# One decoder layer on one core: the attention's steps written in a different order on every engine, W1 loaded early, the last inputs loaded in two parts

## The reference: one decoder layer

```python
def _L0_attn_ref(x, w_qkv, w_out, b_out):        # 16 heads of 8 columns
    qkv = jnp.einsum('bsd,ed->bse', x, w_qkv)
    ...
    q = _apply_rope(q, cos, sin)
    k = _apply_rope(k, cos, sin)
    scores = jnp.einsum('bhsd,bhtd->bhst', q, k) * SCALE
    attn = jax.nn.softmax(scores, axis=-1)
    out = jnp.einsum('bhst,bhtd->bhsd', attn, v)
    out = out.transpose(0, 2, 1, 3).reshape(b, s, d)
    return jnp.einsum('bsd,ed->bse', out, w_out) + b_out

# xattn: an autocorrelation of x and ctx over all batches gives 11 shifts and weights
# ffn: 8 experts (128 -> 256 -> 128), the best 2 of each row, then a layer norm
x = _layernorm(x + _L0_attn_ref(x, ...), axis=-1)
x = _layernorm(x + _L0_xattn_ref(x, ctx_1024, ctx_1024, ...), axis=-1)
x = _layernorm(x + _L0_ffn_ref(x, ...), axis=-1)
```

## Time and profile before

| | |
|---|---|
| median of 3 runs | 232.21 us (231.36 to 234.07) |
| the profiled execution's own time | 231.93 us |
| its span in the profile | 230.1 us |
| PE, weight loads of PE | 214.4 us (93%), 184.0 us (80%) |
| DVE, ACT, POOL | 181.3, 142.5, 111.4 us busy |
| chain of work that ended last | PE 70%, DMA 10%, ACT 6%, DVE 6% |

### The profile page before, as it was taken

The page is one execution under the profiler, slowest core; times in us unless marked ns, Lnnn a source line. Parts: engine busy times, 40 slices in busy tenths (PEclk is TensorE's granted clock), DMA queues, the critical chain, the costliest instruction groups (busy, mean ns, idle before and its releaser), DMA issues.

```text
span 230.1 us, 7213 instructions
## 1 busy us (share of the span) xinstructions
PE 214.4 (93%) x2724; PEld 184.0 (80%) x2724; DVE 181.3 (79%) x622; ACT 142.5 (62%) x248; POOL 111.4 (48%) x219
## 2 busy tenths in 40 slices
PE   7988899999999989998899999999999999999970
PEld 7866677767777666778787999789988999889970
DVE  0688998989899899677744778897798868874885
ACT  2587889989999995574489400891029610596112
POOL 5289879979989995423630400252002600030484
PEclk9999999999999999999999999999999999999996
DMA  5941353975565551610000000001000100001001
GB/s 151 284 119 37 61 107 65 130 156 109 122 139 93 48 91 18 164 36 1 3 0 0 0 3 1 0 3 46 4 0 0 46 3 1 0 4 46 1 16 34
DMA packets 32454, 12.32 MB, mean 54 GB/s; under 512 B 19906, under 2 KB 32290, under 8 KB 32418
## 3 DMA queue, kind: packets, MB, share of 16 engines
q1 hardware_dynamic: 31554, 11.48, 24.2%
q10 hardware_dynamic: 864, 0.36, 0.6%
HBM read 6.33 MB, written 1.05 MB: 32 GB/s over the span
## 4 chain that ended last, share of the span: by engine, by line
PE 70%; DMA 10%; ACT 6%; DVE 6%; issue 4%; SPq 2%; POOL 1%; DVEq 0%; ACTq 0%
PE bank L1328 13%; PE scoreT_pair L1328 12%; PE score_pair L1298 11%; PE scoreT_pair L1298 8%; DMA qT_all<-stack 6%; DMA qT_all<-mT 4%; PE bank L965 4%; PE bank L1042 3%; PE scoreT_pair L997 2%; PE bank L1046 2%; PE scoreT_pair L945 2%; SPq L348 2%; PE bank L1059 2%; ACT early L737 2%; PE score_pair L981 1%
## 5 line engine op out<-in xcount | busy, mean ns | idle before, releaser
L1385 DVE TENSOR_REDUCE rowmax<-score_pair 128x8 f32<-128x1024 f32 x32 | 39.0, 1218 | 4.1 <-PE score_pair L981 3.1
L608 POOL TENSOR_TENSOR ve<-mv,table 128x4 f32<-128x4 f32 (+1 forms) x12 | 3.3, 276 | 78.1 <-DVE mv L1745 60.2
L737 ACT ACTIVATE early<-scoreT_pair 128x1024 f32<-128x1024 f32 x32 | 32.9, 1028 | 6.6 <-PE scoreT_pair L997 6.4
L1328 PE MATMUL bank<-w,early 128*128 128x128 f32 x256 | 30.1, 276 | 0.0
L1328 PE MATMUL scoreT_pair<-w,early 128*128 128x128 f32 x256 | 29.9, 275 | 0.0
L1328 PEld LDWEIGHTS bank<-w,early 128*128 128x128 f32 x256 | 29.5, 192 | 0.3
L1328 PEld LDWEIGHTS scoreT_pair<-w,early 128*128 128x128 f32 x256 | 29.2, 192 | 0.0
L1298 PE MATMUL score_pair<-x2T_part,w_part 128*128 128x512 f32 x108 | 28.4, 397 | 0.0
L880 ACT ACTIVATE early<-score_pair,b 128x512 f32<-128x512 f32 x38 | 26.0, 691 | 3.2 <-PE score_pair L1298 2.6
L1042 PE MATMUL bank<-early,v_pad 128*32 128x128 f32 x512 | 26.5, 279 | 0.4 <-DVE attnT L1401 0.3
L1046 PE MATMUL bank<-early,head_ones 128*32 128x128 f32 x512 | 25.8, 273 | 0.0
(11 more groups left out here) (229 smaller groups left out, 469.6 us busy)
## 6 DMA issues: line engine op xcount, KB each, us to landing
w<-in_w SPq DMA_DIRECT2D x8, 256.0 KB, 3.6
x_ext<-in_x SPq DMA_DIRECT2D x4, 256.0 KB, 6.5
qT_all<-mT SPq DMA_DIRECT2D x32, 32.0 KB, 2.3
early<-in_xT SPq DMA_DIRECT2D x3, 256.0 KB, 4.3
early<-in_ctxT SPq DMA_DIRECT2D x3, 256.0 KB, 5.3
out<-qkv_all SPq DMA_DIRECT2D x3, 256.0 KB, 2.3
table<-in_tables SPq DMA_DIRECT2D x1, 321.0 KB
qT_all<-stack SPq DMA_TRANSPOSE x13, 3.3
```

Of the source, the lines that this page charges most:

```text
L737: act.activation(prob[n % 2][:, 2 * u:2 * u + 2, :, :], scoreT_pair[:, :].rearrange("p (i j s) -> p i j s", i=2, j=QUAD), ACT.Exp, scale=S ...
L1328: mm = pe.matmul(expert_bank[k % 4][:, e4 * D:(e4 + 1) * D], hT[:, f, n * P:(n + 1) * P], w2[:, f, :], start=(c == 0), stop=(c == CH - 1))
L1385: dve.tensor_reduce(rowmax[:, H // 2 * u:H // 2 * (u + 1)], score_pair[:, :].rearrange("p (r t) -> p r t", t=S), AX_X, ALU.max).then_inc(s ...
```

## The change

The change rewrites the order of the calls on PE, ACT, DVE and POOL. The loops over k are written out, and no step is added to or taken from these four engines. On SP the four quarters of W1 move ahead of the b2 blocks, the six small rows go behind three spreads, the x and the context of batches 12 to 15 go behind one spread each, and `q_transpose(4)` changes places with `spread_maxima(2)`.

```diff
+        def load_one(eng, i, which):
+            first, end = LOADS[i]
+            dst, src = ((xT, a["xT"]), (cT, a["ctxT"]))[which]
+            eng.dma_start(dst[:, first:end, :], src[first:end].rearrange("n d s -> d n s")).then_inc(s_x[i], 16)
...
-                if n == 4:
-                    load(sp, 4)
+                if n in (3, 4):
+                    load_one(sp, len(LOADS) - 1, n - 3)
...
-                elif n in (6, 7, 8, 9):
-                    w1_part_in(n - 6)
+                elif n in (6, 7, 8):
+                    for dst, src in late[2 * (n - 6):2 * (n - 5)]:
+                        late_rows(dst, src)
...
+            for i in range(QUAD):
+                w1_part_in(i)
             for n in range(GT):
                 b2_block(n)
-            for dst, src in late:
-                late_rows(dst, src)
...
+            q_transpose(4)
             spread_maxima(2)
-            q_transpose(4)
...
@@ PE
             keep_clock(2)
+            k_transposes(3)
             scoresT(0, 0)
             scores(2, 0)
             maxima_transpose(1)
-            k_transposes(3)
+            qkv(7)
...
+            maxima_transpose(2)
+            scores(3, 0)
+            scoresT(1, 0)
             k_transposes(4)
-            maxima_transpose(2)
-            scoresT(1, 0)
-            scores(3, 0)
-            qkv(7)
             project(0)
...
@@ DVE
             third_piece(dve, 0)
+            keep_turned()
+            remainder(dve, 1)
             residual(0)
-            remainder(dve, 1)
             qT_copy(0)
-            keep_turned()
```

More of the change, by code:

```diff
@@ L797, in _ @@
             kT_copy(4)
+            keep_qkv(7)
             first_piece(6)
-            keep_qkv(7)
+            softmax_exp(2, 0)
             mT_copy(3)
[L801 to L809, removed]
+            second_piece(6)
@@ new lines, in _ @@
+            second_copy(6)
+            keep_qkv(8)
+            softmax_exp(2, 1)
+            kT_copy(5)
+            first_piece(7)
+            softmax_exp(3, 0)
+            mT_copy(4)
+            second_piece(7)
+            keep_qkv(9)
+            second_copy(7)
+            softmax_exp(3, 1)
+            kT_copy(6)
+            first_piece(8)
+            softmax_exp(4, 0)
+            mT_copy(5)
+            second_copy(8)
+            second_piece(8)
+            keep_qkv(10)
+            softmax_exp(4, 1)
@@ L1158, in _ @@
             weighted(1, 1)
+            scores(4, 0)
+            scoresT(2, 0)
+            maxima_transpose(3)
+            qkv(8)
             k_transposes(5)
-            maxima_transpose(3)
-            for k in range(8, 16):
-                scoresT(k - 6, 0)
-                scores(k - 4, 0)
-                qkv(k)
-                project(k - 7)
-                scoresT(k - 6, 1)
-                scores(k - 4, 1)
-                weighted(k - 6, 0)
-                weighted(k - 6, 1)
-                k_transposes(k - 2)
-                maxima_transpose(k - 4)
+            project(1)
@@ new lines, in _ @@
+            scoresT(2, 1)
+            scores(4, 1)
+            weighted(2, 0)
+            weighted(2, 1)
+            scores(5, 0)
+            scoresT(3, 0)
+            maxima_transpose(4)
+            qkv(9)
+            k_transposes(6)
+            project(2)
+            scoresT(3, 1)
+            scores(5, 1)
+            weighted(3, 0)
+            weighted(3, 1)
+            scores(6, 0)
+            scoresT(4, 0)
+            maxima_transpose(5)
+            k_transposes(7)
+            qkv(10)
@@ new lines, in _ @@
+            project(3)
+            scoresT(4, 1)
+            scores(6, 1)
+            weighted(4, 0)
+            weighted(4, 1)
+            scores(7, 0)
+            scoresT(5, 0)
+            maxima_transpose(6)
+            k_transposes(8)
+            qkv(11)
+            scoresT(5, 1)
+            scores(7, 1)
+            project(4)
+            weighted(5, 0)
+            weighted(5, 1)
+            scores(8, 0)
+            scoresT(6, 0)
+            k_transposes(9)
+            maxima_transpose(7)
@@ new lines, in _ @@
+            qkv(12)
+            project(5)
+            scoresT(6, 1)
+            scores(8, 1)
+            weighted(6, 0)
+            weighted(6, 1)
+            scores(9, 0)
+            scoresT(7, 0)
+            maxima_transpose(8)
+            k_transposes(10)
+            qkv(13)
+            project(6)
+            scoresT(7, 1)
+            scores(9, 1)
+            weighted(7, 0)
+            weighted(7, 1)
+            scores(10, 0)
+            scoresT(8, 0)
+            maxima_transpose(9)
@@ L1172, in _ @@
+            k_transposes(11)
+            qkv(14)
+            project(7)
+            scoresT(8, 1)
+            scores(10, 1)
+            weighted(8, 0)
+            weighted(8, 1)
+            scores(11, 0)
+            scoresT(9, 0)
+            maxima_transpose(10)
+            k_transposes(12)
+            qkv(15)
+            project(8)
+            scoresT(9, 1)
+            scores(11, 1)
+            weighted(9, 0)
+            weighted(9, 1)
+            maxima_transpose(11)
             scoresT(10, 0)
@@ L1173, in _ @@
             scores(12, 0)
+            k_transposes(13)
             keep_clock_late(2, qkv_bank, "qkv_kept")
@@ L1201, in _ @@
             weighted(12, 1)
+            project(11)
             scoresT(13, 1)
-            project(11)
             weighted(13, 0)
@@ L1471, in _ @@
             maxima(2, 1)
-            residual(2)
             pieces_of_maxima(dve, 2)
```

311 lines of the change are left out of this document (231 added, 80 removed).

## The result

The changed kernel takes 234.37 us (median of 19 runs, 231.7 to 236.17) against 231.54 us before (19 runs beside them). The ratio is 1.0064, with a 95% interval of 1.0036 to 1.0093: slower by 1.5 us (0.8 to 2.2) by the ratio and by 2.8 us by the medians, where 1.6 us faster than that median was forecast and the range ended at 233.8. Ratios leave out the runs over 1.5% above the fastest of their kernel, which here are four of the 19 (235.77 to 236.17 us, the profiled one among them) and further down one of 350.08 us; the medians keep them. A second set of runs gave 233.69 against 231.61 us, ratio 1.005 (1.0012 to 1.0087).

What follows compares the result with a forecast made beforehand. PE was busy 93% of the span, with four engines near the 5.01 us period, so gains were sought in idle time elsewhere. 231.93 - 0.65 - 1.2 - 1.0 + 0.8 = 229.9 us; the 8-in-10 range was 227.8 to 233.8 us.

Steps and rivals of the forecast that it cites:

- The period: Undisturbed middle iterations: 5.01 us each, with four engines within 0.5 us of that; nothing counted for a change.
- Spreads in the middle: Middle iterations: mT copy now behind the exponential, so spreads land late; 0.2 us lost in four of eight, +0.8 us.
- E + 1.85: Middle iterations: with the exponential at E, the spread's second DMA goes out at about 1.85 us after it.
- One every 10 us on average over the span: Instruction fetching: 22 blocks of 16 KB, one every 10 us, might meet a spread and slow it.
- Four of the eight: Middle: the number of iterations in which a late spread was counted, at 0.2 us each.
- the ring: Middle: exponential, mT copy, spread, scoresT, next exponential; longer than the 5.01 us period once a landing takes over 2.7 us.
- fourth rival: Middle: the spread is late in every iteration, eight iterations of 5.5 us, +3.9 us, total 235.0 us; chance 0.14.
- Iteration k = 10: Two slow middle iterations (5.37, 5.29 us): splitting the x and context loads removes a wait for a transposing DMA, -0.65 us.
- Fill: Start of attention: earlier q_transpose(4) -0.9, moved qkv(7) and k_transposes -0.6, W1's issuing +0.3; together -1.2 us.
- +0.3 us for W1: Fill: issuing W1's four quarters takes 4.6 us on SP and sends the first spread out 0.8 us late, +0.3 us.
- Drain: End of attention: project or k_transposes(13) fills three PE waits for exponentials (0.44, 0.20, 0.38 us), -1.0 us.
- the third one: Rival, gains absorbed: no stall gain at k = 10, fill gains 0.6, half the drain's gain lost, 231.6 us; chance 0.24.

Runs made afterwards that it cites:

- the loads alone: The kernel before with only the change's background loads (W1 at the start, x and context apart, small rows behind spreads): 232.00 us, ratio 0.9995.
- the two kernels with the old middle: Kernel before with the new fill order, DVE's residual(3) moved: 232.11 us; kernel before with the change's fill, drain and loads: 231.18 us.

## Why the prediction was wrong

**The period** was right: iterations without a late spread take 4.95 to 5.01 us in either order.

**Spreads in the middle, +0.8 us on record, +2.8 measured.** This is the step that failed, and by its size alone. The mechanism, E + 1.85 for the second issue, the 2.2 or 3.2 us of landing, were all right (E + 1.86 to 1.89, 2.15, 3.09 to 3.51 measured). Three readings went wrong.

- "One every 10 us on average over the span": a mean over stages. PE issues most of its instructions in the attention. From 38.6 to 74.3 us the trace before has 7 blocks (its q8 row there is below), one each 5.1 us and so about one in each iteration. The row for that was to be had; I read the earlier trace rows over the span and in one window.
- "Four of the eight": five of eight after, and they stand in a row, since the block comes at nearly the same place of each iteration. It isn't drawn anew each time.
- "0.2 us, about half way between 0 and 0.45": a late spread costs its landing less 2.7 us in full, 0.4 to 0.85, because the ring holds everything and nothing makes up for it later. A wait on a ring has no half price.

```profile
q8 instruction: 7, 0.11, 1.3%
```

The five iterations are 3.1 us longer than five of 5.01. My upper bound for the term, 3.6 us, held that; the value that I took lay too near to the other. That the fourth rival's total, 235.0 us, comes near the measured 234.4 is in part luck: it had all eight iterations late, no gain in the fill and all of the drain's. The trace before had the slow landings in plain sight, five in a row of 2.66 to 4.11 us from 39.3 us on, all but one hidden by 1.6 us of slack; I took the earlier trace rows and its 2.2 us for the usual case.

**Iteration k = 10, -0.65 us on record.** Right for the split by itself (the loads alone: 5.01 and 5.00 us in place of the two long ones), and not had in the kernel after. There the long landings, 5.36 and 5.42 us, were those of the transposing DMAs issued at 43.45 and 49.50, now behind context and behind the constants' table; the first piece on ACT waited 0.9 us for the latter, in an iteration that the ring held anyway. The third iteration took 5.28 us with no spread waited for: there ACT's first piece waited 0.4 us for POOL's `rope_sum`, which is on the chain.

**Fill, -1.2 us on record.** -0.84 and -0.95 us in the two profiles of after, -1.08 and -0.98 in the two kernels with the old middle. All are against the slowest of the five unchanged fills, 14.73 us; against their mean of 14.56 it is 0.2 us less. `q_transpose(4)` went out at 25.45 us in the second profile of after (28.86 before) and the exponential (2, 0) started at 32.49, both as the prediction asked. The +0.3 us for W1 was wrong: its four issues took 2.37 us, not 4.6, and SP was done at 17.0 us, against 18.70 before. Of the eight profiles with a short slow stretch at the start (last section), the four with W1 there have the first spread at 18.43 to 19.75 us and the four without at 18.91 to 19.62, so W1 in the fill costs nothing that shows.

```profile
10.49 2.37 SPq L302 DMA_DIRECT2D w<-in_w  x4
12.90 4.12 SPq L334 DMA_DIRECT2D b2d<-in_b  x12
21.06 1.39 SPq L353 DMA_DIRECT2D qT_all<-mT  x2
```

**Drain, -1.0 us on record, between -0.2 and +0.1 measured.** This is the second step that failed, and here it is the mechanism: a wait of PE that is filled was taken for time gained. The waits that I named were filled: `scoresT` waits for the exponential only at 88.95 (0.16 us) and 101.23 (0.38), where the earlier trace rows have 0.44, 0.20 and 0.38 and the wait for the spread stayed (0.78 us, 0.84 before). But filling them moved nothing. From the exponential (10, 0) to (11, 0) both kernels took 4.07 or 4.08 us, from (14, 0) to (15, 1) both 5.06. The chain that ended last goes over ACT there before the change, and after it over DVE:

```profile
79.91 0.36 PE score_pair L1090 x8
80.29 1.24 DVE rowmax L1563
82.17 1.21 DVE rowmax L1563
```

In the second, `project` ahead of `scoresT(15, 0)` made that exponential 0.25 us late (3.54 us behind the one of batch 14, 3.29 before) and the next one as much sooner. ACT, done with its piece, waited for `scoresT` in turn (ACT's timeline):

```profile
98.38 1.02 ACT L790 ACTIVATE early<-scoreT_pair 128x1024 f32<-128x1024 f32 x1 [0.75 <-PE scoreT_pair L1106]
100.15 1.02 ACT L790 ACTIVATE early<-scoreT_pair 128x1024 f32<-128x1024 f32 x1 [0.74 <-PE scoreT_pair L1106]
```

PE's idle time at the waiting instruction was no measure of what filling it is worth. My lower bound, 0, was nearly the answer. What does move the drain is the landing of one spread, that of batch 14 (3.19 us at 89.06 in the earlier trace rows): less that landing, the old order takes 20.32 to 20.40 us in its six profiles and the new one 20.12 to 20.76 in the six without added waits. So the -0.2 us can't be told from 0.

**Sum.** From the first spread on: -0.84 + 2.77 - 0.21 + 0.03 = +1.75 us, where -2.05 stood on record. Of the 3.8 us between them 2.3 are the ring (3.1 in its five iterations, where 0.8 stood on record), 0.3 the rest of the middle, where the third iteration took back part of the stall's gain, 0.8 the drain and 0.4 the fill. The loss is the fourth rival's; that the drain's gain went too is more than the third one had.

## What to carry to other kernels

Where a step is moved, write down the ring that it closes, from an instruction back to itself in the next iteration, and compare its sum with the period for the slowest landing that the trace shows, not for the usual one; what is over counts in full and in every iteration. A slack of 1.6 us that looks unused may be what hides slow transfers. Count an event that comes by instructions (a fetched block) in the stage where the instructions are, not over the span. And a wait of one engine is worth filling only if the engine that it waits for isn't waiting for the same instruction in return.

## What the runs showed of the hardware

**A wait that is already met isn't free on PE.** 128 of them behind the first matmuls ran from 1.1 to 14.8 us, 0.11 us each. The first 3.3 us of that lay beside matmuls, the rest kept PE idle for 10.6 us, where I had expected them to hide. With 192 they ran until 21.9 us, again 0.11 us each, and PE was idle for 17.7. The waits' own row with 128, then PE's timeline:

```profile
L1224 PEldq EVENT_SEMAPHORE  x127: 51/51/51, 1.1 to 14.7; - x127
1.04 3.36 PE L1049 MATMUL bank<-mean_w 128*128 128x128 f32 x14 [1.04 <-DVE mean_w L1619]
15.01 1.62 PE L1068 MATMUL bank<-wqkv,early 128*128 128x384 f32 x2 [10.62 <-issue]
```

**TensorE's first matmuls differ between executions of the same instructions.** Six matmuls in PE's timeline at the start, before, after, and after once more:

```profile
5.97 0.91 PE L945 MATMUL scoreT_pair<-mean_w 128*128 128x128 f32 x6
```

```profile
7.03 1.63 PE L1054 MATMUL scoreT_pair<-mean_w 128*128 128x128 f32 x6
```

```profile
6.22 0.91 PE L1054 MATMUL scoreT_pair<-mean_w 128*128 128x128 f32 x6
```

PE had run the same instructions up to there, and the granted clock reads 1.00, that is 2.4 GHz, for 6 to 8 us in the profiles of before and after alike. After:

```profile
6.00:8.00 2.00, 1.85 (x8) 1.85 (x9) 0.50 (x3) 0.50 (x1) 0.12 (x1) 1.00 0.91 253
```

So the column doesn't show what the durations do. In the profile of after the matmuls stayed slow until about 10.5 us, and the first spread went out at 21.06 us; in that of the same kernel run again it went out at 18.71. Of the twelve profiles without added waits four show the long slow stretch (first spread at 20.85 to 21.40 us) and eight a short one (18.43 to 19.75), with the start as before and with W1 in it alike. So the 2.15 us that the profile of after lost there are an execution's chance. The runs of before look like it: of 100, 67 lie between 230.35 and 232.75 us and 33 between 232.97 and 234.1. What sets it I don't know; no run tested it.
